# A two-layer graph attention with linear attention and eight experts: three row buffers in layer two, heads a batch ahead, the FFN's last layer with nodes on partitions

## The reference

```python
xn = layernorm(x)
x = x + gnn(xn, src, dst) + mix(xn)
x = x + ffn(layernorm(x))
# gnn: two gat_conv (8 heads x 64, then 1 head x 256), elu between them
def gat_conv(x, W, attn_l, attn_r, src, dst, n_nodes):
    feat = (x @ W).reshape(n_nodes, H, D)
    e = leaky_relu(el[src] + er[dst], 0.2)          # el, er = feat . attn
    m = segment_max(e, dst); ex = exp(e - m[dst])
    alpha = ex / segment_sum(ex, dst)[dst]
    return segment_sum(alpha[:, :, None] * feat[src], dst)
# mix: linear attention, 8 heads of 32, phi = elu + 1
# ffn: 8 experts, all of them for every node
w = softmax(mean(x, axis=0) @ Wr + br)              # one row in the batch axis: a gate per node
h = relu(bn(x @ W1[e] + b1[e])); h = relu(bn(h @ W2[e] + b2[e]))
out = sum_e w[e] * (h @ Wo[e] + bo[e])
```

## Time and profile before

| what | us |
|---|---|
| median of 3 runs (lowest, highest) | 4231.7 (4220.61, 4247.79) |
| the profiled execution, its own time | 4219.48 |
| its span in the profile | 4217.7 |
| busy: DVE, POOL, PE, ACT | 2560.0, 2336.9, 2266.2, 1923.2 |
| layer one, from its third batch to 2093.3 | 1589 |
| layer two, batches 0 to 7; 8 to 55 | 208.0; 1356.4 |
| drain of the experts | 166.7 |

### The profile page before, as it was taken

How to read it: one execution, slowest core, us unless ns; L and a number is a source line. 1 busy time by engine, 2 the same in 40 slices (tenths; PEclk the granted TensorE clock), 3 DMA queues, 4 the chain that set the end, 5 groups by cost and what they waited for, 6 DMA issues and landing times. The chain is left out here.

```text
span 4217.7 us, 35862 instructions
## 1 busy us (share of the span) xinstructions
PE 2266.2 (54%) x7342; PEld 1260.4 (30%) x7342; DVE 2560.0 (61%) x5964; ACT 1923.2 (46%) x6163; POOL 2336.9 (55%) x2057
## 2 busy tenths in 40 slices
PE   5930234343333434434345500477877787787799
PEld 3520122222222222222223400233433333343344
DVE  8983677767777667676766624455555555554451
ACT  1200566656665555555533412354444445444443
POOL 0007776667665666676555556555665666565520
PEclk9965666666665555555567755688888888898899
DMA  6321788788887887888754346555555555555520
GB/s 176 96 53 48 258 293 283 280 289 300 301 293 280 280 296 273 295 304 297 256 153 113 97 108 224 159 175 167 187 169 168 175 183 180 181 175 169 175 98 27
DMA packets 282627, 847.01 MB, mean 201 GB/s; under 512 B 73143, under 2 KB 150543, under 8 KB 259102
## 3 DMA queue, kind: packets, MB, share of 16 engines
q0 software_dynamic: 126496, 377.09, 30.3%
q1 hardware_dynamic: 124318, 446.76, 28.4%
q10 hardware_dynamic: 31616, 21.14, 1.8%
HBM read 451.02 MB, written 394.77 MB: 201 GB/s over the span
## 5 line engine op out<-in xcount | busy, mean ns | idle before, releaser
L1295 POOL DMA_INDIRECT e_rows<-scratch_table,k_src x1680 | 1962.3, 1168 | 1053.5 <-DVE e_ring L1395 557.1
L1395 DVE SCALAR_TENSOR_TENSOR e_ring<-e_ring,e_kext,e_rows 128x512 f32<-128x512 f32 (+1 forms) x1568 | 965.7, 616 | 659.0 <-ACT e_rows L1415 355.9
L1415 ACT ACTIVATE e_rows<-e_rows,e_wr 128x64 f32<-128x64 f32 (+1 forms) x4200 | 1208.3, 371 | 8.3 <-issue 3.5
L2064 PE MATMUL e_p_b<-e_h,e_wf 128*128 128x448 f32 x896 | 407.3, 601 | 29.0 <-ACT e_h L1978 24.5
L2052 PE MATMUL e_p_a<-e_xt,e_wf 128*128 128x448 f32 x896 | 387.8, 579 | 28.1 <-ACT e_h L1978 22.6
L2077 PE MATMUL e_p_y<-e_h,e_wfo 128*128 128x448 f32 x896 | 376.9, 562 | 37.1 <-issue 20.6
L1408 ACT ACTIVATE e_wr<-e_d 128x128 f32<-128x128 f32 (+1 forms) x112 | 29.6, 264 | 651.6 <-DVE e_d L1352 427.3
L977 PE MATMUL e_p_c<-e_vext,e_kphi 112*128 112x129 f32 x224 | 62.7, 427 | 435.4 <-DVE e_kphi L867 416.0
L1000 PE MATMUL e_p_q<-k_ident,e_att 112*128 112x112 f32 x112 | 35.5, 421 | 432.0 <-DVE e_att L896 415.2
L1978 ACT ACTIVATE e_h<-e_p_a,e_shift,e_scale 128x448 f32<-128x448 f32 x224 | 154.9, 720 | 247.1 <-remote 152.6
L1978 ACT ACTIVATE e_h<-e_p_b,e_shift,e_scale 128x448 f32<-128x448 f32 x224 | 157.4, 723 | 232.6 <-PE e_p_b L2064 95.1
(11 more groups left out here) (394 smaller groups left out, 3946.5 us busy)
## 6 DMA issues: line engine op xcount, KB each, us to landing
scratch_sums<-e_ring SPq DMA_DIRECT2D x56, 2112.0 KB
scratch_sums<-e_ring SPq DMA_DIRECT2D x56, 1848.0 KB
scratch_sums<-e_ring SPq DMA_DIRECT2D x56, 1032.0 KB
scratch_sums<-e_ring SPq DMA_DIRECT2D x56, 903.0 KB
e_rows<-scratch_table,k_src POOLq DMA_INDIRECT x1680
e_wb<-scratch_gates SPq DMA_DIRECT2D x14, 1792.0 KB
scratch_table<-na_frow ACTq DMA_DIRECT2D x56, 227.5 KB
scratch_table<-hi_frow ACTq DMA_DIRECT2D x56, 115.5 KB
```

The costliest lines, as they stand in the source:

```text
L1295: nc.gpsimd.indirect_dma_start(out=rows[:, n % 2, g, :], out_offset=None, in_=table, in_offset=bass.IndirectOffsetOnAxis(ap=k.src[:, n * G ...
L1395: nc.vector.scalar_tensor_tensor(ring[:, i, j - c0, 0:W], prev, kext[:, 0, j + 1:j + 2], rows[:, b, j, 0:W], ALU.mult, ALU.add).then_inc(s ...
L1415: last = nc.scalar.activation(rows[:, b, j, at], rows[:, b, j, at], ACT.Copy, scale=wr[:, b, h, j + 1:j + 2])
L2064: last = nc.tensor.matmul(self.p_b[mt][:, 0:GN], self.wf2[:, e, kt, mt * P:(mt + 1) * P], self.h1[:, e % 2, kt, :], start=kt == 0, stop=kt ...
```

## The change

1. **Buffers.** Layer two has three row buffers, so the gather of batch n waits for batch n-3. Layer one keeps two.
2. **Heads ahead.** The head of batch n+1 is computed inside batch n: before step j = 12 in layer one, before j = 6 in layer two, with its wait for the rows. It counts on a semaphore of its own (`head_step`).
3. **Tails.** Their pieces move to j = 5, 10, 13 of the round's first batch, and the join to j = 3 of its second; the store of the tails stands ahead of the store of that batch's first half.
4. **FFN's last layer.** Its result has nodes on partitions: the hidden features are the stationary side (128x112), the weights' 256 columns the moving side; eight matmuls of 256 columns per expert for four of 448. Each expert's result is added on DVE by one operation that also multiplies by the gate, which is now a scalar per partition (4 x 112x256 per expert), in place of `weigh_hidden`, the gates' round trip through DRAM, `keep_result` and `turn_result`. The biases come by two matmuls of 512 columns and two additions. PE's output of expert e waits for DVE's additions of e-1 in its bank (`y_added`).
5. **Neighbours.** The e_grow gathers stand one batch later; `join` at j = 7, 10, 11, 13; `norm` at j = 5 of the fourth batch; all four transposes at e = 7; `gates` and `gate_shares` move to the first batch of the next round.

```diff
-L1 = Layer("l1", 8, 512, 4)
-L2 = Layer("l2", 1, 256, 1)
+L1 = Layer("l1", 8, 512, 4, 2, 12)
+L2 = Layer("l2", 1, 256, 1, 3, 6)
...
+    def vector(self, dve, n, j):
+        q = n // PB - 1
+        if q < 0:
+            return
+        at = n % PB * G + j
+        if at == 5:
+            self.vector_scan(dve, q)
+        if at == 10:
+            self.vector_shift(dve, q)
+        if at == 13:
+            self.vector_scale(dve, q)
+        if at == G + 3:
+            self.vector_join(dve, q)
+
+    def scalar(self, act, n, j):
+        q = n // PB - 1
+        if q < 0:
+            return
+        at = n % PB * G + j
+        if at == 11:
+            self.scalar_exp(act, q)
+        if at == G + 11 and q < Q - 1:
+            self.scalar_carry(act, q)
...
                 for i, (c0, c1) in enumerate(HALVES):
+                    if i == 0 and n % PB == 1 and n > PB:
+                        tails.sync_out(sp, n // PB - 1)
                     work.sync(sp, n, i)
-                    if i == 1 and n % PB == 0 and n:
-                        tails.sync_out(sp, n // PB - 1)
...
-                wait(pool, summed, (n - 1) * G)
+                wait(pool, summed, (n - B + 1) * G)
                 for g in range(G):
-                    nc.gpsimd.indirect_dma_start(out=rows[:, n % 2, g, :], out_offset=None, in_=table,
+                    nc.gpsimd.indirect_dma_start(out=rows[:, n % B, g, :], out_offset=None, in_=table,
                                                  in_offset=bass.IndirectOffsetOnAxis(ap=k.src[:, n * G + g:n * G + g + 1], axis=0)
-                                                 ).then_inc(rows_in[n % 2], 16)
+                                                 ).then_inc(rows_in[n % B], 16)
...
+            def head(n):
                 b = n % 2
-                c.block(n, per)
-                c.base = n * per + start
-                dve.wait_ge(rows_in[b], (n // 2 + 1) * 16 * G)
-
-                c(nc.vector.tensor_tensor(z[:, :, :], rows[:, b, :, W:W + H].rearrange("p j h -> p h j"),
-                                          er[:, n * G:(n + 1) * G, 0:H].rearrange("p j h -> p h j"), ALU.add))
-                c(nc.vector.tensor_copy(eext[:, :, 0:1], mext[:, 1 - b, :, G:G1]))
-                c(nc.vector.tensor_scalar(rext[:, :, 1:G1], k.same[:, n * G:(n + 1) * G].unsqueeze(1).to_broadcast([P, H, G]),
-                                          -1.0, BIG, ALU.add, ALU.mult))
-                c.done()
-                c(nc.vector.scalar_tensor_tensor(eext[:, :, 1:G1], z[:, :, :], 0.2, z[:, :, :], ALU.mult, ALU.max))
-                c.done()
-
-                c(nc.vector.tensor_tensor_scan(fext[:, :, :].rearrange(flat), rflat[:, 0:H * G1],
-                                               eext[:, :, :].rearrange(flat), 0.0, ALU.add, ALU.max))
-                c.done()
+                dve.wait_ge(rows_in[n % B], (n // B + 1) * 16 * G)
...
+            head(0)
+            for n in range(NB):
+                b, rb = n % 2, n % B
                 dve.wait_ge(wr_ready, n + 1)
...
                 wait(dve, summed, n * G)
+                wait(dve, den_ready, n)
...
-                        if n % PB == 0 and n:
-                            if j == 2:
-                                tails.vector_scan(dve, n // PB - 1)
-                            if j == 4:
-                                tails.vector_shift(dve, n // PB - 1)
-                            if j == 7:
-                                tails.vector_scale(dve, n // PB - 1)
-                            if j == 10:
-                                tails.vector_join(dve, n // PB - 1)
+                        if j == L.ahead and n < NB - 1:
+                            head(n + 1)
+                        tails.vector(dve, n, j)
...
                 act.wait_ge(d_ready, n + 1)
                 wait(act, summed, (n - 1) * G)
+                wait(act, den_ready, n - 1)
...
-        if n % PB == 1 and n >= PB:
+        if n % PB == 2 and n >= PB:
...
+    def add_result(self, dve, f, e, bank):
         nc = self.nc
-        dve.wait_ge(self.b_kept, self.at(f, e, 1) + 1)
+        dve.wait_ge(self.y_filled, 2 * (f * E + e) + bank + 1)
         if e == 0:
-            dve.wait_ge(self.wb_in, 16 * (f + 1))
-        for mt in range(2):
-            v = self.h2[:, e % 2, mt, :].rearrange("p (i v) -> p i v", i=KB)
-            nc.vector.tensor_tensor(v, v, self.wb[:, :, e, :], ALU.mult).then_inc(self.weighted, 1)
-
-    def add_result(self, dve, f, i):
-        nc = self.nc
-        dve.wait_ge(self.y_turned, KB * f + i + 1)
-        y = self.y[:, f % 3, i, :]
-        nc.vector.tensor_tensor(y, self.p_u[i % 2][0:BK, 0:D], y, ALU.add).then_inc(self.y_added, 1)
+            dve.wait_ge(self.w_ready, f + 1)
+            dve.wait_ge(self.joined, KB * (f + 1))
+        else:
+            dve.wait_ge(self.y_added, 2 * (f * E + e) - 1 + bank)
+        if e == 5:
+            dve.wait_ge(self.bias_added, 2 * f + bank + 1)
+        for i in (2 * bank, 2 * bank + 1):
+            y = self.y[:, f % 3, i, :]
+            last = nc.vector.scalar_tensor_tensor(y, self.p_y[bank][0:BK, i % 2 * D:(i % 2 + 1) * D], self.w[:, i, e:e + 1], y,
+                                                  ALU.mult, ALU.add)
+        last.then_inc(self.y_added, 1)
+
+    def add_bias(self, dve, f, bank):
+        dve.wait_ge(self.bias_filled, f + 1)
+        dve.wait_ge(self.y_added, 2 * (f * E + 4) + bank + 1)
+        y = self.y[:, f % 3, 2 * bank:2 * bank + 2, :].rearrange("p i d -> p (i d)")
+        self.nc.vector.tensor_tensor(y, self.p_u[bank][0:BK, :], y, ALU.add).then_inc(self.bias_added, 1)
...
-        if j == 1 and self.valid((n - 1) // PB - 2):
-            self.weigh_hidden(dve, (n - 1) // PB - 2, 2 * ((n - 1) % PB) + 1)
-        if j == 8 and self.valid(r - 2):
-            self.weigh_hidden(dve, r - 2, 2 * kq)
-        if kq == 1 and self.valid(r - 3) and j in (4, 7, 11, 14):
-            self.add_result(dve, r - 3, (4, 7, 11, 14).index(j))
-        g = r - 1
+        f, g = r - 2, r - 1
+        if j in (1, 2, 8, 9):
+            o, e = (f, 2 * kq - 2) if kq else (r - 3, E - 2)
+            if self.valid(o):
+                self.add_result(dve, o, e if j < 8 else e + 1, (j - 1) % 7)
+        if self.valid(f):
+            if kq == 0 and j == 3:
+                self.gates(dve, f)
+            if kq == 0 and j == 12:
+                self.gate_shares(dve, f)
+            if kq == 3 and j in (3, 4):
+                self.add_bias(dve, f, j - 3)
         if not self.valid(g):
             return
         if kq == 2:
-            if j == 1:
+            if j == 3:
                 self.below(dve, g)
-            if j == 3:
+            if j == 7:
                 self.shares(dve, g)
-            if j in (4, 6, 9, 11):
-                self.join(dve, g, (4, 6, 9, 11).index(j))
-            if j == 13:
+            if j in (7, 10, 11, 13):
+                self.join(dve, g, (7, 10, 11, 13).index(j))
+            if j == 14:
                 self.spread(dve, g)
-        if kq == 3:
-            if j == 2:
-                self.norm(dve, g)
-            if j == 12:
-                self.gates(dve, g)
-            if j == 14:
-                self.gate_shares(dve, g)
+        if kq == 3 and j == 5:
+            self.norm(dve, g)
...
-        pe.wait_ge(self.weighted, self.at(f, e, 1) + 1)
-        for mt in range(2):
-            for kt in range(2):
-                last = nc.tensor.matmul(self.p_y[mt][:, 0:GN], self.wfo[:, e, kt, mt * P:(mt + 1) * P],
-                                        self.h2[:, e % 2, kt, :], start=e == 0 and kt == 0, stop=False,
-                                        skip_group_check=True)
-        if e == E - 1:
-            pe.wait_ge(self.w8_in, 16 * (f + 1))
+        pe.wait_ge(self.b_kept, self.at(f, e, 1) + 1)
+        for bank in range(2):
+            wait(pe, self.y_added, 2 * (f * E + e) - 1 + bank)
+            for i in range(2):
+                v = (2 * bank + i) * BK
+                for kt in range(2):
+                    last = nc.tensor.matmul(self.p_y[bank][0:BK, i * D:(i + 1) * D], self.h2[:, e % 2, kt, v:v + BK],
+                                            self.wfo[:, e, kt, :], start=kt == 0, stop=kt == 1)
+            last.then_inc(self.y_filled, 1)
...
+    def bias(self, pe, f):
+        nc = self.nc
+        pe.wait_ge(self.wt_ready, f + 1)
+        for bank in range(2):
+            last = nc.tensor.matmul(self.p_u[bank][0:BK, :], self.wt[:, :],
+                                    self.bo[:, 2 * bank:2 * bank + 2, :].rearrange("e i d -> e (i d)"), start=True, stop=True)
+        last.then_inc(self.bias_filled, 1)
```

315 lines of the change are left out of this document (133 added, 182 removed).

## The result

The changed kernel took 4702.9 us (median of 4, 4687.5 to 4709.0), the kernel before 4237.8 (4220.6 to 4247.8): a ratio of 1.110, interval 1.105 to 1.115. The forecast was 4207 in a range of 4070 to 4320. The profiled execution spans 4707.2 us, 489.5 more than before. I cut it near the points of the earlier trace rows: layer one at the ends of batches (there at the first instruction of the next head, up to 7 us later), and its second stretch runs to the end of the layer and so holds one batch more. The first eight batches begin 4 us after their first head. Columns as there.

A forecast was written before the change was run, and what follows sets the result against it. Chains of waits, not one engine, were taken to bound the kernel. From the profiled 4219.5 us, +150 (layer one) -27 -150 (layer two) +3 (drain) gave 4195; 12 more for the median gave 4207, range 4070 to 4320.

The forecast's parts named there:

- Layer one, +150: Layer one: with the head before step 12 every batch, not every second, pays for a whole gather; +150 us.
- L: Layer one: time from a gather's start to its rows' landing, forecast 26.6 us in the first half, 27.4 in the second.
- The store beside the gather: Layer one: first half's store issued some 2.7 us earlier, second half's only after the landing, so their collision goes.
- Rival B: Layer two's gain dominates: landing 26 us, layer one +85, a round of layer two 97 us, total 4100; chance 0.32.
- Layer two, -150 and -27: Layer two: -150 us over twelve rounds of 100.5 us each, -27 us in the first eight batches from the third buffer.
- I follow the new chain: Layer two's later rounds: successive waits and batches 41.1 + 17.4 + 17.5 + 21.3, plus 3 for spread, 100.5 us a round.
- E(0): Layer two: end of a round's first batch; the e_grow gathers were forecast to start 9.8 us after it.
- The first eight batches: Start of layer two: the third buffer lets gathers start a batch earlier; -27 us, between -10 and -45.
- The additions with the gate: FFN's last layer: 32 additions on DVE per round at 0.42 us each, +13.4 us of DVE time.
- PE's coupling: FFN: PE's output of an expert waits for DVE's addition of the one before; said to be in the round's sum.
- Rival C: Layer one's gather lands no sooner than 29.5 us, slowed by the first half's store: +275, total 4333; chance 0.18.
- rival D: Layer two: third buffer brings little, DVE's wait at step 6 holds PE, round 108 us, total 4298; chance 0.08.

The follow-up runs named there:

- f4: Changed kernel with layer one's head behind the last step of its batch, on a chip without late PE results: 0.958 of before.
- jobs 1 and 4: Two groups of follow-up runs, each on its own chip, both with late PE results; the kernel before took 4215 and 4226 us there.
- f1: The changed kernel run again with nothing altered, on a chip without late PE results: 1.029 of before, 4165 us.
- e4: The kernel before with a third row buffer in layer two and nothing else: 1.048 of before, 4415 us.
- e3: Changed kernel with GpSimd waiting, in layer two, ahead of a batch's ninth gather until the first eight have landed: 1.057 of before, 4454 us.
- g1: Changed kernel with both heads behind their batch's last step and two buffers in layer two, on a chip with late PE results: 0.994 of before.
- e1: Changed kernel with two row buffers in layer two, head kept at step 6: 1.115 of before, 4696 us.
- f2: The kernel before run again with nothing altered, on a chip without late PE results: 1.001, 4045 us.
- e5: Changed kernel with both heads behind their batch's last step and two buffers in layer two, on a chip without late PE results: 0.961 of before.
- f3: Changed kernel with both heads behind their batch's last step and two buffers in layer two, another chip without late PE results: 0.959 of before.

## Why the prediction was wrong, point by point

- **Layer one, +150 (range +60 to +260): the mechanism was right, the mis-sized term is L, the landing of the gather.** Its own points came true: z waits in every batch (53 times), at step 12, GpSimd 8 to 13 us in each, 10.2 on average. L was 27.6 and 29.2 in the two halves for the 26.6 and 27.4 taken, and the period 33.6 and 34.6 for 32.45 and 32.7. From batch end to batch end that is +111 and +103 for the +82 and +57 that were added up (and 11 for the tails); the first two batches, which the sum left out, bring 15 more. Another thing is not in the sum: with the head at the batch's end the rest of the change would have brought layer one to 1602, so the head costs 295 and something else gains 70. The prediction called the tail work hidden in the idle time before z ("What would hide more isn't there"). It was not: in the trace of before the four batches of a round take 38.2, 24.5, 32.2 and 25.3 us on average, in `f4` 29.3, 29.9, 26.8 and 28.6. Which of the moved tail pieces does this wasn't tried.
- **The store beside the gather.** The first half's store did come earlier, and for its 7 us the gather again moved next to nothing. DMA queues of the changed kernel, 557.8 to 564.8:

```profile
q1 hardware_dynamic: 411, 2.37, 89.3%
q0 software_dynamic: 123, 0.38, 17.6%
```

  Beside the earlier trace rows (393 and 112 packets) it is the same share, and on the chip without lateness too (406 and 127). The Trainium skill, "DMA: Bandwidth & Descriptors", section "Queues, rings and completion order", says that each DMA engine takes turns packet by packet between the queues that have work. If a packet there were a packet of the profile's count, the two counts would be near each other, and no trace here shows that; whether it is, no run shows. Rival B's layer one, L = 26, fell.
- **Layer two, -150 and -27: the step that failed is "I follow the new chain".** Every link of it was taken at the speed at which PE hands over its results in an undisturbed stretch, and the range of 92 to 108 us a round had nothing beyond. In the result the round's second and third batch take 20.9 + 57.2 = 78.1 us for the 58.5 of the chain (41.1 + 17.4), the fourth 20.9 for 17.5, and the next first one 35.2 for 21.3. The e_grow gathers start 8.0 to 8.6 us after E(0), earlier than the 9.8 taken; what is long is what waits for PE behind them. On the chips of the result and of jobs 1 and 4 PE's results are late from some 10 us into a run of gathers until its end. On a chip without this (`f1`) the links hold: 20.0 + 36.0 = 56.0, 15.4 and 21.3, the round 92.8 for a forecast of 100.5 and for 102.9 before, with the wait of z where I looked for it.
- **What in the change brings it out** is shown for the kernel before: the third buffer, counted as a gain, lets 38 gathers run on for 23, and that alone costs 200 us (`e4`). A pause for landed gathers takes the changed kernel's rounds back to 113.1 (`e3`). Inside the changed kernel the parts aren't told apart: with neither the buffer nor the head at step 6 the round is 118.9 (`g1`), with the head alone 132.4 (`e1`), with both 134.2. The buffer without the head at step 6 wasn't tried there. Of the 21.2 us that a round lost, some 6 are then the FFN's and the tails' (118.9 for 113.0, on two chips of the same kind).
- **The first eight batches**, -27 forecast, gained nothing on either kind (+18 in `f1` against `f2`). One of the three waits of the earlier trace rows, 17.6 us, is the one for the layer's first gather, which no buffer makes earlier and which ends where the stretch begins. And the head at step 6 of the eighth batch waits for the ninth gather, so nine must be issued in these batches and not eight: 176.4 and 176.6 us in `f1` and `f4`, 162.9 and 162.2 in `e5` and `f3`, which have no head ahead and two buffers.
- **The additions with the gate** took 0.473 us, near the upper bound of 0.48 and not at the 0.42 taken, 1.7 us a round more; it decides nothing, DVE has room.
- **PE's coupling** (outputs of e wait for additions of e-1) shows as 92.0 us in `f1` in 18 places. It was no term of the sum.
- **Rival C** (slower by layer one, L = 29.5, 4333) had the sign and a place, L being 27.6 and 29.2; rival D had PE standing in layer two (108 a round), by another mechanism. Neither had 4703. On a chip without lateness the change is 1.029, +121 us, where the forecast had -24: 76 of the difference lie in layer one, 45 in the first eight batches and 29 in the later rounds, which gained 121 for 150. The top of the range, 4320, is 1.021 of 4232, so the time lay above it there too.

## What to carry to other kernels

Computing something ahead, in the middle of the previous step's chain, brings its wait along: with two buffers it turned "every second batch waits for a gather" into every batch (295 us). Ask of each new wait what queues behind it and whether that frees the buffer that the wait is for. A row of waits whose releaser had long been done is a question to answer before the forecast: it was the second largest entry of layer two's table, 241.7 us, and a buffer that one adds can feed it. And where a time rests on one chip, run the two kernels on a second.
